# One program for Layer 0: attention, feature attention and the 4-bit feed-forward

## What is computed

```
x = x + attention(layernorm(x))            # 16 heads of 32, one shared key and value head
xn = layernorm(x)
q, k = ctx @ Wq.T + bq, ctx @ Wk.T + bk    # ctx (4, 512, 256), q and k have 128 columns
x = x + einsum('bln,bmn->blm', xn, softmax(q @ k.T))
h = silu(xn2 @ Wgate.T) * (xn2 @ Wup.T)    # xn2 = layernorm(x); 4-bit weights, inner width 1408
x = x + rmsnorm(h @ Wdown.T)
```

## Time and profile before

| | us |
|---|---|
| median of 3 runs (lowest to highest) | 2464.71 (2464.12 to 2466.46) |
| profiled execution | 2463.88 |
| its span | 2461.8 |
| TensorE busy, mean granted clock | 2366.6, 0.988 |
| VectorE, ScalarE busy | 1729.6, 1195.3 |

### The profile page before, as it was taken

The page is one execution under the profiler, slowest core; times in us unless marked ns, Lnnn a source line. Parts: engine busy times, 40 slices in busy tenths (PEclk is TensorE's granted clock), DMA queues, the critical chain, the costliest instruction groups (busy, mean ns, idle before and its releaser), DMA issues. The chain is left out here.

```text
span 2461.8 us, 37463 instructions
## 1 busy us (share of the span) xinstructions
PE 2366.6 (96%) x11266; PEld 1750.7 (71%) x11266; DVE 1729.6 (70%) x3709; ACT 1195.3 (49%) x2341; POOL 159.0 (6%) x281
## 2 busy tenths in 40 slices
PE   7899998899999899999998999999999999999898
PEld 5655556677777688655557777777777777777677
DVE  6578887778887664666757667676667766667873
ACT  3467765433333522477754544444444444444641
POOL 0000000000000000000022010101000101010200
PEclk9999999999999999999999999999999999999999
DMA  5722201000000134433302000000000000001001
GB/s 164 203 75 71 70 18 69 1 1 0 0 0 0 56 120 156 148 93 100 90 30 73 1 13 9 13 9 13 12 9 13 11 11 17 4 9 45 1 18 52
DMA packets 71922, 110.50 MB, mean 45 GB/s; under 512 B 14266, under 2 KB 25274, under 8 KB 71194
## 3 DMA queue, kind: packets, MB, share of 16 engines
q1 hardware_dynamic: 71834, 109.38, 14.5%
HBM read 75.26 MB, written 34.08 MB: 44 GB/s over the span
## 5 line engine op out<-in xcount | busy, mean ns | idle before, releaser
L3378 DVE SCALAR_TENSOR_TENSOR x_res<-xa_out_bank,xa_den,x_res 128x512 f32 (+1 forms) x256 | 191.6, 748 | 140.3 <-PE xa_out_bank L2853 139.7
L3227 ACT ACTIVATE xa_pT_hi<-xa_t_bank 128x512 fp32r<-128x512 f32 x256 | 149.6, 597 | 127.3 <-PE xa_t_bank L3049 127.3
L327 DVE TENSOR_REDUCE l1s_mx<-l1s_max_bank 128x1 f32<-128x512 f32 x256 | 156.4, 680 | 68.5 <-PE l1s_max_bank L185 68.4
L3238 ACT ACTIVATE xa_prob<-xa_prob,xa_nmax 128x512 f32<-128x512 f32 x256 | 182.6, 715 | 29.1 <-DVE xa_nmax L3345 29.1
L3327 DVE TENSOR_TENSOR xa_pT_lo<-xa_t_bank,xa_pT_hi 128x512 fp32r<-128x512 f32 x256 | 175.6, 687 | 23.6 <-ACT xa_pT_hi L3227 23.4
L327 DVE TENSOR_REDUCE l0s_mx<-l0s_max_bank 128x1 f32<-128x512 f32 x256 | 156.8, 680 | 46.6 <-PE l0s_max_bank L185 46.4
L3345 DVE CUSTOM_DVE_ANT_0 xa_prob<-xa_s_bank,xa_mask_bias 128x512 f32<-128x512 f32 x256 | 171.1, 687 | 22.9 <-PE xa_s_bank L2853 11.3
L3031 PE MATMUL xa_bank_a<-xa_xT_hi,xa_q_w 128*128 (+1 forms) x512 | 181.3, 395 | 0.0
L2853 PE MATMUL xa_out_bank<-xa_o_w,xa_o_hi 128*128 128x512 f32 x512 | 170.9, 415 | 8.4 <-DVE x_res L3378 7.3
L2065 DVE SCALAR_TENSOR_TENSOR ffn_yT<-ffn_y,ffn_ysc,ffn_yT 128x512 f32<-128x512 f32 x164 | 120.4, 745 | 42.6 <-PE ffn_y L1799 42.5
L3049 PE MATMUL xa_t_bank<-ident,xa_prob 128*128 128x128 f32 x1024 | 150.0, 274 | 0.1
(11 more groups left out here) (502 smaller groups left out, 5692.2 us busy)
## 6 DMA issues: line engine op xcount, KB each, us to landing
l0s_q<-l_q SPq DMA_DIRECT2D x96, 128.0 KB, 2.4
l1s_q<-l_q SPq DMA_DIRECT2D x96, 128.0 KB, 3.1
l1s_k<-l_k SPq DMA_DIRECT2D x96, 128.0 KB, 3.2
l0s_k<-l_k SPq DMA_DIRECT2D x96, 64.0 KB, 2.4
x_res<-in_x_dram SPq DMA_DIRECT2D x4, 1024.0 KB, 9.4
l_q<-l_q_hi SPq DMA_DIRECT2D x16, 256.0 KB, 2.6
l_q<-l_q_lo SPq DMA_DIRECT2D x16, 256.0 KB, 3.2
l_q<-l_hi SPq DMA_DIRECT2D x16, 256.0 KB, 2.1
```

The costliest lines, as they stand in the source:

```text
L327: dve.tensor_reduce(self.mx[:, j // QT, j % QT:j % QT + 1], self.max_bank[j % 3][:], AX.X, ALU.max)\
L3227: act.activation(pT_hi[:, kt % (QT - 1), :], t_bank[kt % 2][:], ACT.Copy).then_inc(pT_hi_done, 1)
L3238: act.activation(prob[:, q, :], prob[:, q, :], ACT.Exp, bias=nmax[:, q:q + 1], scale=-1.0, accum_out=den[:, r, 0, q:q + 1]).then_inc(exp_d ...
L3378: dve.scalar_tensor_tensor(xt, out_bank[:], den[:, r, 2, q:q + 1], xt, ALU.mult, ALU.add)\
```

## The change

The three stages of Layer 0 become one block. `project_and_attend` and `mix_by_context` no longer open a block; each returns a `Program`, five functions, and `four_bit_ffn` calls them at the head of its own programs. The two pairs of barriers and the clearing of semaphores between them are gone, and where a bank or a tensor passes from one part to the next there is a wait on the semaphore of its last reader.

```diff
 def packed_ffn(st, *args):
     st.ffn_args = args
-    st.stage(project_and_attend, *st.l0_args)
-    st.stage(mix_by_context, *st.fa_biases)
...
+    attend, mixing = project_and_attend(st, *st.l0_args), mix_by_context(st, *st.fa_biases)
+    first_projection, first_exponential, first_normalise = st.before_mix
...
             def _(pool):
+                attend.gpsimd(pool)
...
             def _(sp):
+                attend.sync(sp, st.load_mix_bias)
+                mixing.sync(sp)
...
                 pe.sem_inc(turned, 3)
+                attend.tensor(pe, first_projection)
+                mixing.tensor(pe)
+                st.features_ready(pe)
                 chunk(0, 0)
```

```diff
         self.rounds(pe, step)
+        if before_end:
+            before_end(pe)
         self.turn(pe, self.NP - 1)
...
+        def first_projection(pe):
+            pe.wait_ge(context_turned, CONTEXT_JOBS)
+            project_qk(pe, 0, 0)
...
+        def first_normalise(dve):
+            norm.scales(dve, 0)
+            dve.wait_ge(att.scored, 8 * (att.NP - 2))
+            for q in range(QT):
+                norm.normalise(dve, q)
...
+                if b == 0 and q < 3:
+                    pe.wait_ge(*((att.exp_done, 8 * att.NP), (att.oT_ready, att.NP), (att.o_read, att.NP))[q])
                 ring.turn(pe, at["x", b, q])
```

```diff
+        TURN_CONTEXT = {(3, 8): 0, (3, 10): 1, (2, 0): 2, (2, 2): 3, (2, 5): 4, (2, 8): 5, (2, 10): 6,
+                        (1, 0): 7, (1, 2): 8, (1, 5): 9}
+        TAKE_CONTEXT = {(3, 2): (0, 1), (2, 0): (2, 3), (2, 1): (4,), (2, 2): (5, 6), (1, 0): (7, 8), (1, 1): (9,)}
...
             for kt in range(QT):
                 self.weigh(pe, p, s, kt)
+                if beside and self.late(p, 3):
+                    beside(p, 8 + kt)
...
-        def turn_out_weights(n):
-            if n % 8 >= KC // 2:
+        def turn_out_weights(p, place):
+            j = {(2, 8): 0, (2, 10): 1, (1, 0): 2, (1, 3): 3}.get((att.NP - p, place))
...
-        def take_out_weights(n):
-            for j in range(n * KC // 2, (n + 1) * KC // 2):
+        def take_out_weights(p, place):
+            for j in {(2, 2): (0, 1), (1, 0): (2, 3)}.get((att.NP - p, place), ()):
```

```diff
                 add(b, 1)
+                if not more:
+                    dve.wait_ge(work_read, out_use(b, 0) + 1)
+                    next_stats((12,))
...
+                    next_stats(range(10, 12))
+                    add(b, 3)
+                    pk.norm.combine(dve, 2, batch_tiles(2))
+                    normalise_next(1, range(2, QT))
```

ScalarE, first chunk:

```diff
                         take_x(0)
+                        if b == 0 and first:
+                            norm.root(act, 2, batch_tiles(2))
+                            act.activation(ss[:, 3, 0:1], st.ident[:, 0:1], ACT.Silu)
                         take_x(1)
-                        if b == 0 and first:
-                            norm.root(act, 0, slice(2 * QT, T))
                         silu(c, b)
                         take_x(2)
+                        if b == 1 and first:
+                            norm.root(act, 3, batch_tiles(3))
+                            act.activation(ss[:, 3, 0:1], st.ident[:, 0:1], ACT.Silu)
                         take_x(3)
```

VectorE, first chunk:

```diff
-                        if first and 0 < b < B - 1:
-                            if b == 1:
-                                norm.scales(dve, 0)
-                            normalise(b + 1)
+                        if first and b == 2:
+                            normalise(3, range(1, QT))
...
+                        if first and b == 1:
+                            st.last_added(dve, 0)
+                            norm.tile_stats(dve, T - 2)
                         add_before(0)
                         take_x(0)
+                        if first and b == 1:
+                            st.last_added(dve, 1)
                             norm.tile_stats(dve, T - 1)
                         add_before(1)
                         take_x(1)
                         if first and b == 0:
-                            norm.combine(dve, 0, slice(2 * QT, T))
+                            norm.scales(dve, 2)
+                            normalise(2, range(1))
+                        elif first and b == 1:
+                            norm.combine(dve, 3, batch_tiles(3))
...
                         hidden(c, b, 0)
+                        if first and b == 0:
+                            normalise(2, range(3, QT))
+                        elif first and b == 1:
+                            norm.scales(dve, 3)
+                            normalise(3, range(1))
                         add_before(3)
```

More of the change, by code:

```diff
@@ L12 @@
+from collections import namedtuple
 from contextlib import ExitStack
@@ L57, in stage @@
         self.nc.all_engine_barrier()
-        self.taken = []
+        self.taken, self.chain, self.links = [], None, 0
     def sems(self, *names):
@@ L376, in step @@
                 self.normalise(dve, p - 1)
+                if beside and not reducing:
+                    beside(p, 1)
                 self.add_out(dve, p - 1)
@@ L379, in step @@
                 ahead(p)
+            if beside and self.late(p, 3):
+                beside(p, 2)
         self.rounds(dve, step)
+        if before_end:
+            before_end(dve)
         self.invert(dve, self.NP - 1)
@@ new lines, in load_bias, with sync @@
+        def load_bias(sp):
+            for n, vec in enumerate((bq, bk)):
+                sp.dma_start(bias[:, n:n + 1], column(vec), allow_slow_non_contiguous=True).then_inc(b_loaded, 16)
+        def sync(sp):
+            sp.wait_ge(context_turned, CONTEXT_JOBS)
+            for b in range(B):
+                for part, x in enumerate((ctxT_hi, ctxT_lo)):
+                    sp.dma_start(st.ctx_turned[b, :, part, :, :], x[:, :, b * S:(b + 1) * S].bitcast(F32))\
+                        .then_inc(ctx_stored, 16)
+            sp.wait_ge(b_loaded, 32)
+            sp.wait_ge(ctx_stored, 16 * 2 * B)
@@ new lines, in project_qk @@
+        def project_qk(pe, b, n):
+            u = qk_use(b, n)
+            reached(pe, work_read, u - 1)
+            m = 0
+            for c in range(CC):
+                for w, x in ((wT_hi, ctxT_hi), (wT_hi, ctxT_lo), (wT_lo, ctxT_hi)):
+                    last = pe.matmul(work[n][:], w[:, c, n * P:(n + 1) * P], x[:, c, b * S:(b + 1) * S],
+                                     start=(m == 0), stop=(m == 3 * CC - 1))
+                    m += 1
+            last.then_inc(worked, 1)
+        def first_projection(pe):
+            pe.wait_ge(context_turned, CONTEXT_JOBS)
+            project_qk(pe, 0, 0)
@@ new lines, in first_exponential, with scalar, take_qk, exponential @@
+        def first_exponential(act):
+            act.activation(warm[:], st.ident[:, 0:1], ACT.Exp)
+        def scalar(act):
+            def take_qk(b, n):
+                if b == 0:
+                    act.wait_ge(b_loaded, 32)
+                act.wait_ge(worked, qk_use(b, n) + 1)
+                act.activation(hi[n][:], work[n][:], ACT.Identity, bias=bias[:, n:n + 1]).then_inc(hi_done, 1)
+            def exponential(b, q):
+                act.wait_ge(nmax_ready, QT * b + q + 1)
+                act.activation(prob[b % 2][:, q, :], energy[(QT * b + q) % 3][:], ACT.Exp,
+                               bias=nmax[:, q:q + 1], accum_out=den[:, q:q + 1]).then_inc(exp_done, 1)
+            def normalise(b, rows):
+                act.wait_ge(rden_done, b + 1)
+                for q in rows:
+                    act.activation(prob[b % 2][:, q, :], prob[b % 2][:, q, :], ACT.Identity,
+                                   scale=rden[:, q:q + 1]).then_inc(prob_ready, 1)
+            take_qk(0, 0)
+            take_qk(0, 1)
+            for q in range(3):
+                ring.take_hi(act, at["x", 0, q])
+            for q in range(3):
+                exponential(0, q)
+            ring.take_hi(act, at["x", 0, 3])
+            exponential(0, 3)
+            normalise(0, range(2))
+            ring.take_hi(act, at["w", 0])
+            for b in range(B):
+                more = b + 1 < B
+                if more:
+                    take_qk(b + 1, 0)
+                ring.take_hi(act, at["a", b, 0])
+                if b == 0:
+                    ring.take_hi(act, at["w", 1])
+                elif b == 2:
+                    norm.root(act, 1, batch_tiles(3))
+                    pk.norm.root(act, 0, batch_tiles(0))
+                if more:
+                    take_qk(b + 1, 1)
+                for k in range(1, QT):
+                    ring.take_hi(act, at["a", b, k])
+                if more:
+                    for q in range(QT):
+                        exponential(b + 1, q)
+                    normalise(b + 1, range(2))
@@ L2143, in chunk, with normalise @@
                             (magnitudes, exponents)[b - 2](c + 2)
-                def normalise(b):
-                    for q in range(QT):
-                        if b > 1:
```

(4 more changed lines are left out.)

1181 lines of the change are left out of this document (562 added, 619 removed).

## The result

| | before | changed |
|---|---|---|
| median (lowest to highest) | 2464.41 (2462.23 to 2466.46), 4 runs | 2446.98 (2444.98 to 2448.06), 4 runs |
| profiled execution, its span | 2463.88, 2461.8 | 2444.98, 2443.2 |
| TensorE busy, clock | 2366.6, 0.988 | 2354.3, 0.993 |
| VectorE, ScalarE busy | 1729.6, 1195.3 | 1730.4, 1197.0 |

Two more measurements of the same kernel, on other chips, gave 0.9936 [0.9922 to 0.995] and 0.9939 [0.9927 to 0.9951], which is 15.8 and 15.0 us; the medians themselves lie 12.8 and 14.7 us apart. So the gain is 13 to 17 us: the sign and the mechanism were right, the size was not.

A forecast was written before the change was run, and what follows sets the result against it. TensorE, busy 96% of the span, bounds the kernel, so time is won where it stands or runs at half clock. 1.5 + 5.95 + 5.1 - 0.9 = 11.6 us gave 2453.1, range 2451 to 2455 (chance 0.57).

The forecast's parts named there:

- Part 1: Layer 0's attention tail: context turns moved partly behind value products; 3.1 us less against 1.65 paid, net 1.5 gained.
- Part 2: First hand-over, attention to feature attention, without its barrier: 5.2 us instead of 11.15, so 5.95 gained.
- Rival A: First hand-over: the last pair's chain, not TensorE, sets feature attention's start and moved turns gain nothing; 2456, chance 0.15.
- Part 3, standing time: Second hand-over, feature attention to 4-bit feed-forward: the 2.95 us in which TensorE stands go.
- Rival C: At one or both hand-overs a wait replacing the barrier holds TensorE about as long: 2459 to 2462, chance 0.08.
- Part 3, the first three batches: Feed-forward's start: first batch 8.0 to 8.4 us instead of 10.75, 2.3 gained; second and third 0 net.
- Part 4: Layer 1: two of four out-weight turns go behind value products of pair 30; 0.9 us lost.
- Rival B: First feed-forward chunk: ScalarE's table switches take two loads' time more, 2.6 us, before the last x; 2455.7, chance 0.15.
- Rival D: Feed-forward chunk 0: several short waits drop the clock for batches two and three, 19.3 us more; 2472, chance 0.02.
- the better side of part 3: Second and third feed-forward batches: both waits for normalised tiles come free, +2.8 us; 2450, chance 0.03.

The follow-up runs named there:

- b_att: The kernel before with only the two tensors of turned scores placed ahead of the normalised tiles, as in the changed kernel: 2463.16, ratio 1.0001.
- a_swap: Changed kernel with Layer 1's out weights turned where they were and the second batch's last x copied before batch 3's root and Silu reload: 2448.48, ratio 0.9939.
- a_norm_old: Changed kernel with the feed-forward norm's old order for VectorE, ScalarE and the last mixing batch: 2454.16, ratio 0.9957.
- a_stop2: Changed kernel with block end and two barriers put back between feature attention and feed-forward, semaphores not cleared: 2455.73, ratio 0.9966.
- a_two_more: Changed kernel with one more Sqrt and one more Silu of a single column behind batch 3's root in the first chunk: 2455.3 in one execution.

## Why the prediction was wrong in size

**Part 1 was right, by luck: two errors cancel.** Net 1.4 to 1.8 for 1.5. The scores of pairs 30 and 31 came down to ScalarE's pace, 4.3 and 4.1 like the earlier trace rows, not to 4.9 and 4.6: the 0.45 for a third turn was not there, 4.2 us gained in place of 3.1. Against it the value products with turns between them take 4.6 and 5.1 us (347.06 to 351.68, 355.99 to 361.05) instead of 3.6, so 2.5 us in place of 1.65.

**Part 2 was right.** 6.1 for 5.95. ScalarE's two loads start at 366.36, directly behind the last exponential, and it is through at 369.4. That is 0.6 us behind the last value product's end (368.77), where the prediction had 0.2 to 0.3 (370.4 and 370.15), and it held nobody: the last output is turned only behind the first projection, at 370.19. Rival A's late chain shows in one wait of 0.31 us, where the rival had 1.5. What the prediction did not see is that only 3.6 of the 6.1 are the barrier; 1.4 are the new order and 1.1 a half-clock window that `b_att` loses with the barrier in place.

**Part 3, standing time: right.** 3.1 for 2.95; VectorE's last low half is in time, as reckoned. Rival C, a wait that takes the barrier's place, didn't come: 0.31 us is the longest of TensorE's waits at either.

**Part 3, the first three batches: the term that failed.** "2.3 first batch, 0 net for the two others" measured 4.3. By batches 7.66, 10.60 and 10.34, where I had 8.4, 11.2 and 11.0: each 0.6 to 0.8 too long. The mechanism held: combination, root, Silu, x, low half in this order, and the gate waits 1.09 us for it. The sizes did not. In the first batch I took the upper end of "8.0 to 8.4", without a sum for it; TensorE was busy for 7.54 of 7.66. In the third I added 0.7 for hidden values and 0.4 for a turn to 9.88 of work; it worked 10.08 and stood 0.26, of which 0.19 are the wait for the normalised tile, and none is for the hidden values. For the second batch the rows show the place. VectorE's timeline in it:

```profile
472.80 0.68 DVE L449 TENSOR_TENSOR ffn_xB_lo<-ffn_turn,ffn_xB_hi 128x512 fp32r<-128x512 f32 x1
473.39 0.68 DVE L490 BATCH_NORM_STATS2 ffn_bn<-x_res 128x6 f32<-128x512 f32 x1
473.99 0.73 DVE L2121 TENSOR_SCALAR ffn_yT<-ffn_y,ffn_ysc 128x512 f32<-128x512 f32 x1
474.64 0.68 DVE L449 TENSOR_TENSOR ffn_xB_lo<-ffn_turn,ffn_xB_hi 128x512 fp32r<-128x512 f32 x1
475.24 0.15 DVE L498 TENSOR_TENSOR ffn_mv<-ffn_bn 128x4 f32<-128x4 f32 x1
```

Instructions of 0.68 us start 0.60 apart: neighbours overlap by 0.08. The combination was done 7.5 us into the batch, not 8.1, and everything behind it (x at 9.73, not 10.45) came earlier by that much. How much of the 0.6 is the overlap in my sum and how much an instruction placed too late the runs don't separate. Before against after, what went in the three batches is 2.9 us of standing (32.91 - 28.50 = 4.4 to 28.60 - 27.13 = 1.5) and 1.4 us of clock; the forecast had nearly all of the clock and little of the standing, since it let the second and third batch give back what they gained. They gave back 1.09, in the wait that `a_swap` removes, and 0.26 in the third. And the forecast had no term for what happens when only one of the two edits is made: that the gain of this hand-over hangs on both at once (7.4 us, against 1.1 and 1.4) only `a_norm_old` and `a_stop2` show.

**The mixing, taken as unchanged, gave 2.3.** The placement of the turned scores stood in the change, and I put it at nothing with the other small edits: 0.7 by the stretches. The other 1.6 are a fall of the clock that this execution of the changed kernel did not have and its copies have. The first of these is a missed term. The second is luck; the prediction named it as something that may shift by one, either way. The 2.2 us in stretches whose work is the same are luck of the two executions too.

**Part 4 was right**, 0.7 to 0.9 for 0.9. **Rival B** fell with `a_two_more`: the loads cost what the row shows. **Rival D** did not come in the changed kernel, but `a_norm_old` shows the mechanism it described: behind a wait of 2.42 us the clock falls, a second wait of 1.36 lies in the fall, and the clock is 0.74 on average over the batch. It costs 2.5 us there and not 19.

Put together: 11.6 + 2.1 (batches) + 0.7 (placement) + 0.3 (small ones) = 14.7. The copies agree with it: 15.8 and 15.0 by their ratios, 12.8 and 14.7 by their medians. With 1.6 for the fall near the third mixing batch and 2.2 elsewhere it makes the 18.5 to 18.6 between the two profiled executions. The range was too narrow above all because it let the better side of part 3, bounded at 2.8, count for 3 chances in 100.

## What to carry to other kernels

When a barrier between two stages goes, work out the order behind it anew: at the second hand-over the fusion alone gave 1.1 us, the new order alone 1.4 and both 7.4, since the chain for the last operand of the next batch had been covered in part by the barrier's own delay. And part of what looks like a barrier's price (here 1.4 of 6.1 us) is order, to be had without a fusion. Sum a chain by start-to-start distances in the timeline, not by durations, and leave more room on the side where several waits may all come out free.

## What the hardware showed

- The same product with its operand at another address was 4 to 5 ns of 394 to 398 shorter, in 192 products of three forms (`b_att` against before).
- A table load on ScalarE takes 1.28 us, without a drain, and starts before the wait of the function that needs it: in `a_two_more` the 0.23 us of standing for VectorE lie behind the load, not ahead of it.
- After the same wait of 1.61 us the clock fell in before and in both copies of the changed kernel and not in the changed kernel's own profile: between executions of one program such a fall comes and goes, 1.6 us each time.
